# A two-attention, two-feed-forward kernel: the first attention drained in another order, the second one begun inside the feed-forward

## What is computed

```python
x = x + attn_a(layernorm(x))   # 16 heads of 64, causal softmax, output projection
x = x + ffn(layernorm(x))      # routed slots, below
x = x + attn_b(layernorm(x))   # within each token, its 16 heads of 8 attend to each other
x = x + ffn(layernorm(x))      # the same weights again

# attn_a: q, k, v = x @ wq, wk, wv; softmax(mask(q k^T / 8)) v; heads joined @ wo.T
# attn_b: q, k, v = x @ Wq.T, Wk.T, Wv.T; per token a 16 x 16 softmax over heads;
#         the result is laid out (head, token, 8), read as (256, 128), @ Wo.T + bo
# ffn:    h = gelu([x, slot_mean] @ w1 + b1); logits = (h @ w2 + b2) / (|tau| + 0.1)
#         alpha = softmax over the 8 largest of 64 logits, zero elsewhere
#         slot_input = alpha^T x / sum(alpha); a GRU step with slot_init
#         attention among the 64 slots; layer norm; values; out = alpha @ values @ wo + bo
```

## Time and profile before

| | us |
|---|---|
| median of 3 runs | 886.03 (884.98 to 886.19) |
| the profiled execution | 888.32 |
| its span, first to last instruction | 886.2 |
| TensorE busy | 779.7 (88%) |
| VectorE busy | 652.8 (74%) |
| ScalarE busy | 482.5 (54%) |
| GpSimd busy | 418.3 (47%) |
| mean granted clock | 0.958 |

### The profile page before, as it was taken

How to read it: one execution, slowest core, us unless ns; L and a number is a source line. 1 busy time by engine, 2 the same in 40 slices (tenths; PEclk the granted TensorE clock), 3 DMA queues, 4 the chain that set the end, 5 groups by cost and what they waited for, 6 DMA issues and landing times.

```text
span 886.2 us, 25741 instructions
## 1 busy us (share of the span) xinstructions
PE 779.7 (88%) x10372; PEld 599.7 (68%) x10372; DVE 652.8 (74%) x1528; ACT 482.5 (54%) x853; POOL 418.3 (47%) x326
## 2 busy tenths in 40 slices
PE   1899999999999999999999896957899999959695
PEld 0688888888888888888888765534455555535554
DVE  3676667666766676677668777635999999998754
ACT  1587668667866686767676452313344444424331
POOL 1354444444444444444446320013898888893000
PEclk9999999999999999999999996988999999977699
DMA  7000000000000000000000000000122222121002
GB/s 292 1 3 1 0 0 0 0 0 0 0 0 0 0 0 0 0 0 0 0 0 3 1 1 1 1 0 1 13 25 24 24 24 24 19 25 18 1 1 95
DMA packets 71589, 13.26 MB, mean 15 GB/s; under 512 B 66432, under 2 KB 70528, under 8 KB 70912
## 3 DMA queue, kind: packets, MB, share of 16 engines
q1 hardware_dynamic: 71552, 12.76, 6.6%
HBM read 8.56 MB, written 4.19 MB: 14 GB/s over the span
## 4 chain that ended last, share of the span: by engine, by line
PE 66%; DVE 15%; ACT 7%; issue 6%; POOL 3%; DMA 2%; DVEq 0%; SPq 0%; ACTq 0%; POOLq 0%
PE PS L572 6%; PE PS L529 6%; PE PS L361 5%; PE PS L362 4%; PE PS L363 4%; PE PS L441 4%; DVE b_prod L895 3%; PE PS L565 3%; PE PS L551 3%; POOL b_w L943 2%; PE PS L780 2%; PE PS L770 2%; DVE a_nm L655 2%; PE PS L967 2%; PE PS L536 2%
## 5 line engine op out<-in xcount | busy, mean ns | idle before, releaser
L688 POOL TENSOR_TENSOR a_pl<-a_p,a_ph 128x1024 f16<-128x1024 f32 (+1 forms) x128 | 210.5, 1645 | 258.9 <-ACT a_ph L601 258.9
L943 POOL TENSOR_TENSOR b_w<-b_v,b_e 128x2048 f32<-128x2048 f32 x32 | 137.9, 4309 | 13.0 <-ACT b_e L861 13.0
L598 ACT ACTIVATE a_p<-PS 128x1024 f32<-128x1024 f32 (+1 forms) x128 | 103.8, 811 | 73.7 <-PE PS L536 73.6
L655 DVE TENSOR_REDUCE a_nm<-PS 128x4 bf16<-128x512 f32 (+1 forms) x128 | 121.4, 949 | 0.1
L591 ACT ACTIVATE a_qk_h<-PS 128x512 f16<-128x512 f32 x128 | 73.4, 604 | 58.2 <-PE PS L363 57.0
L601 ACT ACTIVATE a_ph<-PS 128x1024 f16<-128x1024 f32 (+1 forms) x128 | 103.1, 805 | 0.0
L895 DVE TENSOR_TENSOR b_prod<-PS,b_qt 128x512 f32<-128x512 f32 x128 | 80.3, 678 | 18.3 <-PE PS L772 17.6
L644 DVE TENSOR_TENSOR a_qk_l<-PS,a_qk_h 128x512 f16<-128x512 f32 x128 | 87.0, 681 | 3.4 <-ACT a_qk_h L591 3.4
L384 POOL TENSOR_TENSOR veps<-mv,eps 128x2 f32<-128x2 f32 (+1 forms) x52 | 11.2, 215 | 148.3 <-DVE mv L1244 119.8
L361 PE MATMUL PS<-xhl,a_wqk_h 128*128 128x256 f16 x256 | 71.3, 279 | 8.3 <-ACT xhl L589 7.5
L551 PE MATMUL PS<-a_vh,a_ph 128*128 128x65 f16 x768 | 77.6, 195 | 0.1
(11 more groups left out here) (232 smaller groups left out, 2027.4 us busy)
## 6 DMA issues: line engine op xcount, KB each, us to landing
scratch_dram<-b_o SPq DMA_DIRECT2D x32, 64.0 KB, 4.1
b_y<-scratch_dram SPq DMA_DIRECT2D x16, 128.0 KB, 2.0
out_dram<-X SPq DMA_DIRECT2D x2, 1024.0 KB, 3.9
w_rest<-rest_dram SPq DMA_DIRECT2D x1, 1862.0 KB, 15.2
X<-x_dram SPq DMA_DIRECT2D x1, 1792.0 KB, 11.2
w_first<-first_dram SPq DMA_DIRECT2D x1, 1600.0 KB, 6.9
w_rolls<-rolls_dram SPq DMA_DIRECT2D x1, 544.0 KB, 15.5
X<-x_dram SPq DMA_DIRECT2D x1, 256.0 KB, 3.4
```

The costliest lines, as they stand in the source:

```text
L598: act.activation((a_p0, a_p1)[j][:, me, :, :, :].rearrange("p a h q -> p a (h q)"), TT[:, :, 0:512 - 256 * j], ACT.Exp, scale=EA ** -0.5)
L655: dve.tensor_reduce(a_nm[:, nx, j, :].rearrange("p (a h) -> p a h", a=2)[:, :, 0:2], MM[:, :, 0:256 * (j + 1)].rearrange("p a (h k) -> p a ...
L688: pool.tensor_tensor(*(n[:, g % 2, :, :, :].rearrange("p a h q -> p (a h q)") for n in (pl, p, ph)), ALU.subtract).then_inc(a_split, 1)
L943: pool.tensor_tensor(b_w8[:, j, :, :, :], rolled_values(par, j, 0, H), rolled_exps(par, j, 0, H), ALU.mult).then_inc(b_weighed, 1)
```

## The change

Nothing that is computed changes; steps of the plans move, and two waits move with them.

- **Last sequence of the first attention.** `ffn_stats` of quads 0 and 1 now both stand late in g = 1, after the second row maximum, and those of quads 2 and 3 in the epilogue. `ffn_apply` 0 and 1 move from g = 2 to g = 3; 2 and 3 stay in the epilogue, further back, the last behind the final addition. `set_mm` 0 moves from the end of g = 3 to behind the last `pv`, and `set_ev` 0 behind the last `normal`; `set_mm` 1 stands between the last `turn` and `end`.
- **Feed-forward.** A new step `lead` on DVE, between `values` 1 and `add` 1, makes the statistics of sequence 0 of the second attention; DVE's own `norm` of that sequence is dropped. It is left out in the second feed-forward.
- **Opening of the second attention.** The whole preparation of sequence 1 is spread among the rolls of sequence 0; roll 1 goes ahead of `v`, rolls 4 and 5 ahead of `dots` 0.
- **Waits.** Those for `consts_set` move to the first router matmul and the first Gelu. Roll 2 of sequence 0, the first to write a bank of chunk 1, now waits for that chunk's additions.

```diff
@@ -78,7 +78,7 @@
         put(True, ("maxrow", 0))
         put(prepare, ("lo", 0))
         put(not (first and g < 2), ("normal", 0))
-        put(last and g == 2, ("ffn_apply", 0))
+        put(last and g == 3, ("ffn_apply", 0), ("ffn_apply", 1))
         put(prepare, ("lo", 1), ("masks", 0))
         put(g == 1 and not last, ("apply", 0))
         put(True, ("later", 0), ("exps", 0))
@@ -88,19 +88,16 @@
         put(begun, ("pv", 0), ("pv", 1))
         put(not (first and g < 2), ("turn", 0))
         put(prepare, ("vlo", 0))
-        put(last and g < 2, ("ffn_stats", 2 * g))
-        put(last and g == 2, ("ffn_apply", 1))
         put(g == 0 and not last, ("norm", 0))
         put(g == 2 and not last, ("renew", 0))
         put(prepare, ("masks", 1))
         put(True, ("later", 1))
         put(prepare, ("max", 1))
-        put(last and g < 2, ("ffn_stats", 2 * g + 1))
+        put(last and g == 1, ("ffn_stats", 0), ("ffn_stats", 1))
         put(True, ("exps", 1), ("exph", 1))
-        put(last and g < 2, ("ffn_rstd", 2 * g), ("ffn_rstd", 2 * g + 1))
+        put(last and g == 1, ("ffn_rstd", 0), ("ffn_rstd", 1))
         put(g == 1 and not last, ("xt", 0))
         put(g == 1 and not first, ("project", 0))
-        put(last and g == 3, ("set_mm", 0))
     return steps
 
 
@@ -144,14 +141,13 @@
 
 A_PROLOGUE = [("norm", 3, 0), ("apply", 3, 0), ("xt", 3, 0), ("renew", 3, 0), ("qk", 3, 0), ("qk", 3, 1), ("lo", 3, 0),
               ("lo", 3, 1), ("masks", 3, 0), ("max", 3, 0), ("v", 3, 0), ("vlo", 3, 0), ("masks", 3, 1), ("max", 3, 1)]
-A_EPILOGUE = [("normal", 0, 0), ("turn", 0, 0), ("set_ev", 0, 0), ("begin", 1, 0), ("ffn_apply", 0, 2), ("ffn_apply", 0, 3),
-              ("pv", 0, 0), ("pv", 0, 1), ("set_mm", 1, 1), ("more", 1, 0), ("normal", 1, 0), ("set_ev", 1, 1), ("turn", 1, 0),
-              ("end", 1, 0)]
-B_PROLOGUE = [("norm", 0, 0), ("apply", 0, 0), ("xt", 0, 0), ("xlow", 0, 0), ("qk", 0, 0), ("klow", 1, 0), ("early", 1, 0),
-              ("v", 1, 0), ("values", 1, 0)]
-for m in range(ROLLS):
-    B_PROLOGUE += [("roll", 1, m)] + ([("dots", 1, m // 4)] if m % 4 == 3 else [])
-B_PROLOGUE += [("flip", 1, 0), ("flip", 1, 1), ("norm", 1, 0), ("apply", 1, 0), ("xt", 1, 0), ("xlow", 1, 0), ("qk", 1, 0)]
+A_EPILOGUE = [("normal", 0, 0), ("turn", 0, 0), ("begin", 1, 0), ("ffn_stats", 0, 2), ("ffn_stats", 0, 3), ("ffn_rstd", 0, 2),
+              ("ffn_rstd", 0, 3), ("pv", 0, 0), ("pv", 0, 1), ("set_mm", 1, 0), ("more", 1, 0), ("normal", 1, 0), ("set_ev", 1, 0),
+              ("turn", 1, 0), ("ffn_apply", 0, 2), ("set_mm", 1, 1), ("set_ev", 1, 1), ("end", 1, 0), ("ffn_apply", 0, 3)]
+B_PROLOGUE = [("norm", 0, 0), ("apply", 0, 0), ("xt", 0, 0), ("xlow", 0, 0), ("norm", 1, 0), ("qk", 0, 0), ("klow", 1, 0),
+              ("early", 1, 0), ("apply", 1, 0), ("roll", 1, 0), ("roll", 1, 1), ("v", 1, 0), ("values", 1, 0), ("roll", 1, 2),
+              ("roll", 1, 3), ("roll", 1, 4), ("roll", 1, 5), ("dots", 1, 0), ("xt", 1, 0), ("roll", 1, 6), ("xlow", 1, 0),
+              ("roll", 1, 7), ("dots", 1, 1), ("flip", 1, 0), ("flip", 1, 1), ("qk", 1, 0)]
 B_EPILOGUE = [("project", 0, 0), ("finish", 0, 0), ("add", 0, 0), ("yt", 0, 0), ("gather", 0, 1), ("normal", 0, 0),
               ("ffn_apply", 0, 0), ("ffn_apply", 0, 1), ("ffn_rstd", 0, 2), ("ffn_rstd", 0, 3), ("ffn_apply", 0, 2),
               ("ffn_apply", 0, 3)] + [("ffn_stats", 0, q) for q in (4, 5, 6)] + [("ffn_rstd", 0, q) for q in (4, 5, 6)] + [
@@ -187,8 +183,8 @@
           ("inputs", 0), ("wih", 0), ("alpha", 1), ("gates", 0), ("candidate", 0), ("read", 1), ("new", 0), ("slots", 1),
           ("qkv", 0), ("inputs", 1), ("scores", 0), ("wih", 1), ("gates", 1), ("probs", 0), ("candidate", 1), ("attend", 0),
           ("new", 1), ("qkv", 1), ("values", 0), ("scores", 1), ("out", 0), ("probs", 1), ("attend", 1), ("add", 0),
-          ("values", 1), ("out", 1), ("add", 1)]
-EARLY = [[], [(kind, q) for kind in ("stats", "apply") for q in (4, 5, 6)] + [("split", 0), ("hidden", 0), ("set", 0)]]
+          ("values", 1), ("out", 1), ("lead", 0), ("add", 1)]
+EARLY = [[], [("lead", 0)] + [(kind, q) for kind in ("stats", "apply") for q in (4, 5, 6)] + [("split", 0), ("hidden", 0), ("set", 0)]]
 
 
 class Fill:
@@ -766,6 +762,8 @@
                     if j == 0:
                         pe.wait_ge(b_lo, b + 2)
                     wait(pe, b_multiplied, m - 1 if j < 2 else m - 2)
+                    if isinstance(b, int) and b == -1 and j == 2:
+                        pe.wait_ge(f["added"], CHUNKS * 4)
                     for e in range(2):
                         pe.matmul(ROLLED[j % 3][:, e * SEQ:(e + 1) * SEQ], w["roll"][:, 2 * j + e, :], b_kh[:, nx, :],
                                   start=e == 0, stop=False, skip_group_check=True)
@@ -883,7 +881,7 @@
                     if kind == "ffn_stats":
                         dve.wait_ge(b_added, 2 * j + 2)
                     norm_quad(dve, link, kind, 1, j)
-                elif kind == "norm":
+                elif kind == "norm" and (not isinstance(i, int) or b > -2):
                     wait(dve, b_rstd, b + 2)
                     norm_stats(dve, link, X, (b + 2) * QT, QT).then_inc(b_stats, 1)
                 elif kind == "roll":
@@ -963,6 +961,8 @@
 
         def router(pe, c, k, n):
             pe.wait_ge(f["xt_ev"], (k - 1) * GROUPS + n + 1)
+            if k == 1 and n == 0:
+                pe.wait_ge(consts_set, 1)
             wait(pe, f["gelu"], (k - 1) * GROUPS + n - 1 if (c or n >= 2) else 0)
             pe.matmul(PS[4 - 2 * c + n % 2][0:DH, :], w["w1a"][:, :], f_xt[:, n * 512:(n + 1) * 512],
                       start=True, stop=True).then_inc(f["h_mm"], 1)
@@ -992,7 +992,7 @@
 
         def f_tensor(pe, rep):
             def do(kind, c, k):
-                if kind in ("stats", "apply", "split"):
+                if kind in ("stats", "apply", "split", "lead"):
                     return
                 if kind == "set":
                     return set_tensor(pe, 2)
@@ -1101,13 +1101,15 @@
                 if n == 0 and c:
                     act.wait_ge(f["logit_mm"], k - 1)
                 if n >= 1:
+                    if k == 1 and n == 1:
+                        act.wait_ge(consts_set, 1)
                     act.wait_ge(f["h_mm"], (k - 1) * GROUPS + n)
                     act.activation(f_h[0:DH, (n - 1) * 512:n * 512], PS[4 - 2 * c + (n - 1) % 2][0:DH, :],
                                    ACT.Gelu, bias=c1[:, :]).then_inc(f["gelu"], 1)
 
         def f_scalar(act, rep):
             def do(kind, c, k):
-                if kind in ("stats", "apply", "split", "set"):
+                if kind in ("stats", "apply", "split", "set", "lead"):
                     return
                 v = chunk[c]
                 B = f_banks(c)[0]
@@ -1162,6 +1164,10 @@
                     return norm_quad(dve, link, "ffn_" + kind, rep, c)
                 if kind in ("split", "set"):
                     return set_vector(dve, link, 2 + (kind == "set"))
+                if kind == "lead":
+                    dve.wait_ge(f["added"], 4)
+                    norm_stats(dve, link, X, 0, QT).then_inc(b_stats, 1)
+                    return
                 v = chunk[c]
                 B, L = f_banks(c)
                 if kind == "topa":
@@ -1374,7 +1380,6 @@
         def _(act):
             act.wait_ge(dve_set, 1)
             a_scalar(act)
-            act.wait_ge(consts_set, 1)
             f_scalar(act, 0)
             b_scalar(act)
             f_scalar(act, 1)
@@ -1403,7 +1408,6 @@
             pe.wait_ge(pool_set, 1)
             pe.wait_ge(dve_set, 1)
             a_tensor(pe)
-            pe.wait_ge(consts_set, 1)
             f_tensor(pe, 0)
             b_tensor(pe)
             f_tensor(pe, 1)
```

## The result

The changed kernel takes 871.91 us (871.80 to 874.01, 3 runs) against 886.03 before: a ratio of 0.9852, 95% interval 0.9832 to 0.9872, 14.1 us less.

The account below looks back on a forecast made before the run. VectorE bounds the second attention's bulk; the first attention's drain and the second's opening are chains of waits. Drain -3.7 and opening -9.6 take the median from 886.0 to 872.7, said as 873; 8-in-10 range 869.0 to 878.0.

Parts of the forecast that it names:

- The drain: Last sequence and drain of the first attention: statistics, applications, clock, later turn and constants together -3.7 us.
- Statistics: Drain: without statistics of quads 0 and 1 in g = 0, TensorE waits less for the row maximum; -1.5 us.
- Applications: Drain: applications 0 and 1 leaving g = 2 bring the row maximum earlier, the exponentials being late next; -1.4 us.
- The clock's 1.0: Drain, weighted values: with a gap under one us, TensorE's clock does not fall to 0.50; gain 1.0 us.
- The 0.4 for the later turn and the 0.2 for the constants: Drain: applications in g = 3 make the next turn 0.4 us late; the constants, moved but not hidden, are worth 0.2.
- The feed-forward: First feed-forward: same work, same order, only earlier; TensorE's slack of 3.4 us covers application 2's 1.1; moved waits met.
- The opening: Second attention's opening: start -4.1, rolls of sequence 0 -0.7, between the sequences -4.2, rolls of sequence 1 -1.0 us.
- The 0.4 given back for ScalarE's queue: Opening: ScalarE's apply, values and copies of two sequences stand in one queue; 0.4 us given back, leaving -9.6.
- One, the exclusion in g = 3,: Rival, drain: moved applications wait for GpSimd's split of 1.15 us, the turn is late by 1.15: 874.2; chance 0.08.
- Two, absorbed,: Rival: the drain's gain is lost to VectorE's quads 4 to 7 and constants, or another low clock: 876.4; chance 0.12.
- Three, the clock,: Rival: whole opening at 1.00 and one low stretch of the feed-forward gone: 870.4, or 869 without roll stalls; chance 0.11.
- Four and five: Rivals: GpSimd's late products cancel the opening's gain, 886 with a lost drain, 0.04; steady loop's 11.45 period grows, 891, 0.03.

## Why the prediction was right, point by point

**Forecast and sum.** 873.0 was said and 871.9 measured; the sum of differences was -13.3, and -14.4 came in the span. No rival was needed. That the two are so close is in part cancellation: the drain gave 0.8 more than forecast and the opening 0.4 more, the feed-forward took 0.6 back that wasn't in the sum, and 0.5 came in stretches that the change doesn't touch.

**The drain: mechanism right, term too small.** -3.7 was said, -4.5 came. Statistics: -1.5 and -1.62, with the isolated change giving the same; TensorE's start moved by 0.89, the 0.9 of the sum, and the copy behind it by the rest. Applications: -1.4 and -1.84. That step took the exponentials as what is late next; TensorE in fact started at 492.67 behind the maximum as before, with 0.96 of its wait left, and it also no longer waited 0.28 for a split. The clock's 1.0 was about right in this pair, by luck as far as the runs show: with the gap of 2.33 back, the clock stayed at 1.00 behind it and was low for longer in the feed-forward. The 0.4 for the later turn and the 0.2 for the constants were 0.35 and 0.27.

**The feed-forward: this step failed.** "The rest of the feed-forward is the same work in the same order, only earlier" and "this slack covers the 1.1". The slack of 3.4 us was that of the first transposes of chunk 1. The second ones need a bank that VectorE frees behind application 7, and there the slack was about 0.3 against a delay of 0.9. It cost 0.6. The moved wait in front of the Gelu held TensorE back by the same 0.6 at the same place; that it would have cost them by itself, without the new drain, is argued and not run. "Met" was true of the wait and not of the table load, which stood idle for the router's result.

**The opening: right in each term.** -4.1, -0.7, -4.2 and -1.0 were said, -4.27, -0.43, -4.20 and -1.13 came. The second goes with the clock: the same order took 6.95 to 7.55 us, -0.1 to -0.7. The 0.4 given back for ScalarE's queue wasn't needed. Reading the 4.85 us between two sequences off the next pair, instead of adding it up, was the best number of the forecast: 4.88. The first transpose and `xlow` ran at full clock and the fall came behind them, as expected.

**The rivals.** *One, the exclusion in g = 3,* missed by little: GpSimd's split ended at 492.92 + 1.16 = 494.08 and the applications started at 494.04 and took 2.13, their length without company. With them back in g = 2, where the split runs 0.89 into application 1, it took 1.74 again. The prediction's "plus four pitches of 0.28 is its end" doesn't come out: 494.35 and 1.12 are 495.47, and the application ends at 495.20. By a closer window of the same trace the first of its four instructions takes 0.97 instead of 0.34 and ends 0.08 behind the split; the other three follow at their usual distance. The Trainium skill (SBUF — State Buffer, section "Who interferes with whom") gives the rule; the trace agrees in all four executions that have the overlap, the kernel before and three experiments, each with 1.74. *Two, absorbed,* was real for 0.6 of 4.5. *Three, the clock,* didn't come in the opening: TensorE fell to 0.50 there as well. *Four and five:* GpSimd is done 0.83 before the second `gather`, and the period is 11.45 as before.

## What to carry to other kernels

A step that is ready early costs nothing only at the place in the queue where its engine idles anyway: the same statistics cost 1.6 us in one group of heads and nothing in the next. Slack must be taken at each thing that the late engine delivers, not at the first; and where two limits lie side by side, removing one alone can show nothing. When executions of one kernel differ by more than the term in question, cut the traces at fixed steps and compare the cuts.

## What the runs showed of the hardware

An activation that needs another table had its table load behind TensorE's result when two waits stood in front of it: 0.72 us idle before the load. With one wait the load followed the copy at once. A VectorE `tensor_scalar` that began while GpSimd's split ran took 0.97 us instead of 0.34 and ended 0.08 behind the split. And TensorE's clock behind the same gap of 2.33 us, in front of the same weighted values, fell to 1.2 GHz in three executions and stayed at 2.4 in one.
